# Softmax exponentials per head on ScalarE with the negated maximum as bias, without the subtraction on VectorE

## The reference

```
h = tok(x, mask)
h = h + attn0(layernorm(h))      # 12 heads of 16 features
h = h + moe(layernorm(h))
h = h + attn1(layernorm(h))
h = h + fff(layernorm(h))

# attn0, per token block of 64 keys
q = (x @ Wq.T + bq) * SCALING
scores = einsum('bqd,bkd->bqk', q, k)
probs  = softmax(scores.astype(float32), axis=-1)
attn   = einsum('bqk,bkd->bqd', probs, v)

# attn1, 128 keys
attn = softmax((attn_scores + rel_scores) * scale, axis=-1)
out  = einsum('bhts,bhsd->bhtd', attn, v)
```

## Time and profile before

| | us |
|---|---|
| median of 3 runs | 2292.38 |
| lowest, highest | 2286.29, 2294.81 |
| profiled execution, own time | 2303.16 |
| its span | 2301.4 |
| PE busy | 1939.5 (84%) |
| DVE busy | 1398.7 (61%) |
| ACT busy | 1011.9 (44%) |
| POOL busy | 582.0 (25%) |

### The profile page before, as it was taken

The page is one execution under the profiler, slowest core; times in us unless marked ns, Lnnn a source line. Parts: engine busy times, 40 slices in busy tenths (PEclk is TensorE's granted clock), DMA queues, the critical chain, the costliest instruction groups (busy, mean ns, idle before and its releaser), DMA issues. The chain is left out here.

```text
span 2301.4 us, 57092 instructions
## 1 busy us (share of the span) xinstructions
PE 1939.5 (84%) x18472; PEld 1759.0 (76%) x18472; DVE 1398.7 (61%) x3153; ACT 1011.9 (44%) x2767; POOL 582.0 (25%) x1167
## 2 busy tenths in 40 slices
PE   4999999999500068999999999699999999999985
PEld 4888888888300058999999999598888888888872
DVE  6777777776432233555555545477777777777735
ACT  2555555555100022333333333366666666666621
POOL 4333333342057700000000000433333333333100
PEclk9999999999655579999999999799999999999957
DMA  5222122221012278788888787465555555555513
GB/s 140 60 60 63 55 62 56 61 56 32 10 64 77 77 217 252 231 229 229 240 231 235 230 231 211 134 177 157 159 160 162 162 159 158 157 160 162 150 30 110
DMA packets 377516, 322.51 MB, mean 140 GB/s; under 512 B 55451, under 2 KB 338031, under 8 KB 377455
## 3 DMA queue, kind: packets, MB, share of 16 engines
q1 hardware_dynamic: 357790, 287.75, 43.7%
q0 software_dynamic: 15360, 31.48, 4.6%
q10 hardware_dynamic: 4304, 2.49, 0.4%
HBM read 210.03 MB, written 111.60 MB: 140 GB/s over the span
## 5 line engine op out<-in xcount | busy, mean ns | idle before, releaser
L1128 ACT ACTIVATE prob<-ps_s,b1s 128x256 f32<-128x256 f32 x432 | 181.7, 472 | 369.4 <-PE ps_s L1112 369.4
L1112 PE MATMUL ps_s<-xhi,w1hi_c 128*128 128x256 f32 x864 | 239.3, 295 | 2.6 <-DVE xhi L1150 2.6
L1112 PE MATMUL ps_s<-xhi,w1lo_c 128*128 128x256 f32 x864 | 229.6, 284 | 0.0
L1075 PE MATMUL ps_t<-ident,xs 128*128 128x128 f32 x144 | 38.1, 291 | 213.0 <-DMA score<-w1h 212.6
L1087 PE MATMUL ps_v<-probT,prob 128*128 128x192 f32 x864 | 214.1, 330 | 0.0
L1087 PE MATMUL ps_k<-probT,prob 128*128 128x192 f32 x864 | 213.5, 329 | 0.0
L1142 DVE CAST w1hi_c<-score 128x768 fp32r<-128x768 f32 x144 | 74.1, 557 | 225.0 <-DMA score<-w1h 225.0
L373 PE MATMUL ps_k<-xT,wqk_c 128*128 128x128 f32 x1408 | 194.5, 288 | 0.6 <-ACT xT L608 0.6
L424 PEld LDWEIGHTS ps_v<-vv,probT 128*128 128x128 f32 x1536 | 189.0, 198 | 1.1 <-issue 1.0
L1075 PEld LDWEIGHTS ps_t<-ident,xs 128*128 128x128 f32 x144 | 20.6, 143 | 220.6 <-DMA score<-w1h 205.5
L424 PE MATMUL ps_v<-vv,probT 128*128 128x17 f32 x1536 | 187.6, 261 | 0.5 <-DVE hres L676 0.5
(11 more groups left out here) (209 smaller groups left out, 4746.2 us busy)
## 6 DMA issues: line engine op xcount, KB each, us to landing
rel_d<-rpad SPq DMA_DIRECT2D x64, 864.0 KB, 4.4
relb<-rel_d SPq DMA_DIRECT2D x64, 768.0 KB, 5.0
probT<-w2h SPq DMA_DIRECT2D x72, 576.0 KB, 4.1
score<-w1h SPq DMA_DIRECT2D x72, 384.0 KB, 3.2
score<-w1h SPq DMA_DIRECT2D x144, 192.0 KB, 3.9
xs_d<-zrow SPq DMA_DIRECT2D x64, 216.0 KB, 2.8
xs<-xs_d SPq DMA_DIRECT2D x72, 192.0 KB, 2.5
ys_d<-ys SPq DMA_DIRECT2D x72, 192.0 KB, 4.9
```

The lines of the kernel that those rows point to most:

```text
L1075: pe.transpose(ps_t[:, s * 128:s * 128 + 128], xs[b][:, s, 0:128], ident[:])
L1112: last = pe.matmul(dst, w, x, start=(k == 0), stop=(k == len(terms) - 1))
L1128: last = act.activation(hT[b][:, c, :], ps_s[:, j, (c % 2) * BLK:(c % 2) * BLK + BLK], ACT.Gelu, bias=b1s[b][:, c:c + 1])
```

## The change

The subtraction on DVE and the buffer write that went with it are removed. After the maximum, DVE writes -SCALE times the maximum into a small tile `nmx` (12 columns) and signals s_max. ACT computes twelve exponentials per tile, one per head, each with the head's column of `nmx` as bias: exp(SCALE * s - SCALE * max). In layer 0 it reads the scores from PSUM, in layer 1 from `score`. In layer 1 they stand where the one exponential stood. In layer 0 they stand one step earlier, between the two copies of transposed probabilities, and PE's next scores wait for p_sb, since it is now ACT that reads ps_s last.

```diff
-                    after(pe, S["s_rd" if l == 1 else "s_sub"], before("s"))
+                    after(pe, S["s_rd" if l == 1 else "p_sb"], before("s"))
...
-                if st.has("pt"):
-                    b = st.two("pt")
-                    act.wait_ge(S["s_sub"], done("pt"))
-                    act.activation(prob[b][:, 0:H * keys].rearrange("p (g a k) -> p g a k", g=G, a=A),
-                                   score[b][:, :, :, 0:keys], ACT.Exp, scale=SCALE).then_inc(S["p_sb"], 1)
+                def exponentials(k):
+
+                    b = st.two(k)
+                    act.wait_ge(S["s_max"], done(k))
+                    for h in range(H):
+                        g, a = h // A, h % A
+                        part = ps_s[:, g, a * keys:(a + 1) * keys] if l == 0 else score[b][:, g, a, :]
+                        ins = act.activation(prob[b][:, h * keys:(h + 1) * keys], part, ACT.Exp,
+                                             bias=nmx[b][:, h:h + 1], scale=SCALE)
+                    ins.then_inc(S["p_sb"], 1)
+
+                if l == 1 and st.has("pt"):
+                    exponentials("pt")
...
                 if st.has("pt"):
                     turned_probs(0)
+                if l == 0 and st.has("s"):
+                    exponentials("s")
+                if st.has("pt"):
                     turned_probs(1)
...
                     ch.link(dve.tensor_reduce(mx[b][:].rearrange("p (g a) -> p g a", g=G), src, AX.X, ALU.max))
+                    dve.tensor_scalar(nmx[b][:], mx[b][:], -SCALE, None, ALU.mult).then_inc(S["s_max"], 1)
...
-                if st.has("s"):
-                    b = st.two("s")
-                    m4 = mx[b][:].rearrange("p (g a o) -> p g a o", g=G, o=1).to_broadcast([128, G, A, keys])
-                    dve.tensor_tensor(sc, src, m4, ALU.subtract).then_inc(S["s_sub"], 1)
```

More of the change, by code:

```diff
@@ L231, in tower @@
         mx = two("mx", [128, H])
+        nmx = two("nmx", [128, H])
         prob = two("prob", [128, H * 128])
@@ L277, in tower @@
                  "xT_sb", "q_ps", "q_sb", "k_ps", "k_sb", "r_ps", "r_sb", "v_ps", "v_sb", "s_ps",
-                 "s_rd", "s_sub", "p_sb", "pt_ps", "pt_sb", "o_ps", "o_sb", "oT_ps", "oT_sb", "y_ps", "y_ok",
+                 "s_rd", "s_max", "p_sb", "pt_ps", "pt_sb", "o_ps", "o_sb", "oT_ps", "oT_sb", "y_ps", "y_ok",
                  "mvz_ok", "rsz_ok", "zn_ok", "zT_ps", "zT_sb", "lg_ps", "lg_sb")
```

## The result

The changed kernel takes 2527.57 us (median of 4 runs, 2521.79 to 2533.91) against 2293.6 us of the kernel before: ratio 1.1024, 95% interval [1.0998, 1.1049], so 234 us more. Forecast were 2468 us in a range of 2425 to 2535. The direction and the two places were right; the size was low by 59 us, and the result lies 7 us inside the upper end of the range. All medians in this document are of fast executions: three executions of the experiments whose granted clock was 0.52 to 0.78, against 0.90 to 0.93 in all others, are left out.

What follows compares the result with a forecast made beforehand. The prediction took per-tile rings of waits as the bound, with PE close to full. From 2303.16 us profiled, adding 52 (layer 0), 113 (layer 1) and 11 (clock) gave 2479, less 10.8 for the median 2468 us; stated range 2425 to 2535.

Steps and rivals of the forecast that it cites:

- two rings through ACT: Waits closing once per tile: PE's next scores wait for ACT in layer 0, PE's output projection in layer 1.
- Layer 0's ring after the change: PE's scores to ACT's copy 6.80 us, copy 0.38, twelve exponentials 2.62, handover to PE 0.14: 9.94 us per step.
- Layer 0's step before: Layer 0's step in the old kernel: 9.14 us mid-stage with DVE's subtraction in the way, 8.65 us in four late steps.
- Layer 1's ring: Twelve exponentials hold ACT 3.36 us instead of 1.37, PE's slack is 0.17: 1.82 us more per step, 113 us over 62.
- Distance per head in layer 0: Start-to-start time of layer 0's biased 64-column exponentials from PSUM: 0.21 us, bounds 0.12 and 0.31.
- The clock: New PE pauses in layer 1 lower the clock in one step of eight, 1.4 us each: 11 us.
- Full overlap: Rival 1: a bias costs no start-to-start time; layer 0 gives back 17 us, layer 1 costs 24, about 2299 us; chance 0.04.
- no overlap: Rival 3: exponentials don't overlap, costing 122 us in layer 0 and 195 in layer 1, about 2620 us; chance 0.06.
- The faster case: Rival 2: layer 0 bound by PE alone, 29 us less, and layer 1's block fits 1.54 us; about 2263 us; chance 0.02.
- Rival 4: Clock falls in nearly every layer 1 step, and in layer 0: 2544 us, up to some 2630; chance 0.12.

Runs made afterwards that it cites:

- the run with filled pauses: Changed kernel plus unread matmuls in PE's new pauses, six before layer 1's output projection, four at the end of layer 0's steps: 2488.79 us, ratio 1.0863.
- with one exponential: Changed kernel with one maximum over all 12 heads of a row, so one biased exponential per tile: 2290.83 us, ratio 0.9977 to the kernel before.

## Why the prediction was right, and where it was off

- **What bounds.** Right: two rings through ACT, closed in layer 0 by PE's scores and in layer 1 by the output projection. Placing the blocks elsewhere moves the time as these rings say.
- **Layer 0's ring after the change.** 9.94 forecast, 9.88 measured; each of its terms within 0.06 us.
- **Layer 0's step before.** This term was wrong. I took 9.14 us from the earlier trace rows for 59 steps, and 8.65 us for the four late ones only, and put the difference down to the embedding, which the late steps lack. The kernel before has 8.65 us in three steps of four, all through layer 0, with the embedding. Four starts of PE's scores in its timeline, 8.64, 8.65 and 9.01 us apart:

```profile
315.99 0.32 PEld L357 LDWEIGHTS ps_s<-kT,qT 32*64 32x64 f32 x24 [0.20 <-issue]
...
324.63 0.32 PEld L357 LDWEIGHTS ps_s<-kT,qT 32*64 32x64 f32 x24 [0.20 <-issue]
...
333.28 0.32 PEld L357 LDWEIGHTS ps_s<-kT,qT 32*64 32x64 f32 x24 [0.20 <-issue]
...
342.29 0.35 PEld L357 LDWEIGHTS ps_s<-kT,qT 32*64 32x64 f32 x24 [0.56 <-issue]
```

And on DVE, the instruction behind the loop's jump (the loop body holds four steps):

```profile
334.59 0.38 DVE L684 TENSOR_SCALAR xn<-hres,mvb,rs 128x192 f32 x1 [0.56 <-issue]
```

DVE is idle for 0.56 us there, once in every four steps, and only in that step is its subtraction late for PE (by 0.32 us, as in the earlier trace rows). From query copy to query copy three steps last 8.65 us and the fourth 9.15, so the mean step is (3 x 8.65 + 9.15) / 4 = 8.78 us, and the ring costs 1.10 us per step, not 0.80: 60 steps make 66 us, where I had 47 + 5 = 52 in all. Two rows one step apart had stood for a stage; three more steps of the same line would have told.
- **Layer 1's ring.** 1.82 us per step forecast, 13.59 - 11.69 = 1.90 measured. The exponentials' distance was 3.51 / 12 = 0.292 us, not 0.28, which is +0.15 per step; the step of before was 11.69 on average, not 11.60, -0.09.
- **Distance per head in layer 0.** 0.21 forecast, 2.35 / 12 = 0.196 measured (320.36 to 322.71 above). The estimate from the figures of the Trainium skill ("ScalarE: Activation LUTs", section "What ACT_TABLE_LOAD costs") was 0.24 us, and 0.29 in layer 1: the trace agrees in layer 1 (0.292) and is well under it in layer 0 (0.196), where the source is PSUM.
- **The clock.** Mis-sized: 11 us forecast for layer 1 and none for layer 0, against 19 + 13 in the steps of the profile, and as much in the run with filled pauses. I had the price of a stretch (1.4 us; steady steps show 1.3 to 1.6 for each, twice that where two stretches join) and took too few. In layer 0 the sum has the clock at nothing and gives no reason for it; the pause of 1.33 us in the earlier trace rows had not brought it down, but pauses of 1.17 us did, in one steady step of six.
- **Rivals.** Full overlap is refuted by the distances, no overlap too (0.196 under a duration of 0.36). The faster case needed a block under 1.33 us; with one exponential it is 0.91 and this case does come true, at -5 us. Rival 4 was right that layer 0 falls too, but not in its number of steps: nine slow stretches in 62 steps of layer 1, not nearly all. (Its 2570 for half of the steps of layer 0 is a slip: 2544 + 44 = 2588.)
- **Sum.** The 59 us come in two parts. The profiled executions are 218.6 us apart, where the forecast had 52 + 113 + 11 = 176: 43 us. Layer 0 grew by 86: 66 for the steps, 13 for the clock, and some 7 in its first and last steps; against the 52 forecast that is 14 for the step of before and 7 for the first and last ones. The clock is 21 (32 for 11). Layer 1 grew by 130, of which 19 the clock; the other 111 are 2 less than the 113 forecast, since the first and last steps don't pay the 1.90 us in full. The other stages add 3. The remaining 16 us are no term of the kernel: I took the median to lie 10.8 us below the profiled execution, as before, and the changed kernel's lies 5.8 above it. Which stage makes an unprofiled execution longer no run shows.
- **The range.** The number held because the stated range went up to 2535, with 40 us for the clock. The mechanism was right in both layers, while errors of 14, 21 and 16 us all went the same way; with one more of that size the measurement would have been outside.

## What to carry to other kernels

A broadcast operation on a wide tile that is replaced by a bias per slice turns one instruction into many, and each costs its fixed part, of which 0.09 us is the bias from memory; count instructions on the engine that takes the work over, then look which ring their block lies in, before counting what the other engine saves. A block that can't be made shorter can often be moved beside the other engine's work: here the places alone were worth 120 of 234 us. Read the length of a step over several turns of the loop, and ask of every new pause on TensorE what the clock does after it.

## What the runs showed of the hardware

- ACTIVATEs of 64 columns from PSUM with a bias start 0.196 us apart but last longer from one to the next, 0.318 us for a tile's first and 0.409 for its twelfth, so their ends are 0.204 us apart; at 128 columns from SBUF they all last 0.40 and start 0.292 us apart.
- Less 0.83 ns per column, the distance has a fixed part of 0.143 us in layer 0 (from PSUM) and 0.186 in layer 1 (from SBUF) with a bias, 0.050 and 0.093 without. It is the same with one, four or twelve instructions per tile, so it goes with the layer and its source, not with the columns; source and layer were not varied separately.
- A pause of 1.17 us per step of 9.88 us brought the clock down in one steady step of four to six (four profiles), one of 0.80 us in none (two profiles), and in layer 1 one of 1.7 us in a step of 13.6 in about one of seven. A stretch at 1.2 GHz lasted 3.4 us or twice that. Dummy matmuls in the pause kept the clock up; the kernel was 1.5% faster than without them, 31 of the 39 us of it in the stages that they stood in.
